# Third cross-attention of a four-layer Perceiver: the symmetric head sums in four column tiles of 32, between the next chunk's projections

## What is computed

```python
def proj(t):                       # 8 heads of 128
    return (layer_norm(t, ln_g, ln_b) @ w_in.T).reshape(Q, N, H, D).transpose(2, 0, 1, 3)
f_q, f_k, f_v = proj(q), proj(k), proj(v)          # k and v are the same context
cosine_sim = einsum('hqnd,hqmd->hqnm', f_q, f_k) / (norm(f_q)[..., None] * norm(f_k)[:, :, None])
k_ratio = 2.0 * minimum(var(f_k), 1.0) / (var(f_k) + 1.0)
var_component = einsum('hqn,hqm->hqnm', q_ratio, k_ratio)
mixed = cw * cosine_sim + vw * (cosine_sim * decorr_scale) + ww * var_component
out = einsum('hqnm,hqmd->hqnd', mixed, f_v)        # then @ w_out.T + b_out
```

## Time and profile before

| | |
|---|---|
| median of 3 runs | 2513.9 us (2513.67 to 2517.24) |
| the profiled execution's own time | 2512.27 us |
| its span | 2510.4 us |
| TensorE busy | 2241.1 us, 89% |
| VectorE busy | 1830.1 us, 73% |
| ScalarE busy | 1176.9 us, 47% |
| GpSimd busy | 520.0 us, 21% |
| mean granted TensorE clock | 0.944 |
| from the first projection of the stage to the last sums | 1421.7 to 1913.3 us of the span |

### The profile page before, as it was taken

One profiled execution on the slowest core, in us unless ns is written; L12 is line 12 of the kernel. 1 busy time (PEld: TensorE's weight loads), 2 busy tenths in 40 slices (PEclk: granted clock), 3 DMA queues, 4 the chain that ended last, 5 costly groups with the idle time before them and its releaser, 6 DMA issues. The chain is left out here.

```text
span 2510.4 us, 56943 instructions
## 1 busy us (share of the span) xinstructions
PE 2241.1 (89%) x21794; PEld 1438.2 (57%) x21794; DVE 1830.1 (73%) x2832; ACT 1176.9 (47%) x2049; POOL 520.0 (21%) x300
## 2 busy tenths in 40 slices
PE   2999979999996969999987999999998459999979
PEld 1444436666665936666666646665556425556548
DVE  6888778999996176676634488888887877777721
ACT  4566643443435337767772333333331415556542
POOL 0555540000000030000001065556662010000000
PEclk7999989999997969999998999999998769999989
DMA  8577755766745767667735322222222257777654
GB/s 282 201 242 242 261 197 148 203 200 171 206 147 179 228 154 170 161 167 172 170 71 180 128 103 103 103 102 95 75 71 62 84 131 164 157 167 176 155 142 175
DMA packets 245978, 398.00 MB, mean 159 GB/s; under 512 B 28921, under 2 KB 210305, under 8 KB 245669
## 3 DMA queue, kind: packets, MB, share of 16 engines
q1 hardware_dynamic: 240132, 393.90, 54.3%
q10 hardware_dynamic: 5664, 1.44, 0.3%
HBM read 316.44 MB, written 78.06 MB: 157 GB/s over the span
## 5 line engine op out<-in xcount | busy, mean ns | idle before, releaser
L1713 ACT ACTIVATE l1x_prob<-l1x_ring,mask_col 128x512 f32<-128x512 f32 x392 | 248.6, 690 | 113.6 <-PE l1x_ring L1805 113.3
L1629 DVE CUSTOM_DVE_ANT_0 l3x_junk<-l3x_pm,l3x_mrow,l3x_top 128x896 bf16<-128x896 f32 x224 | 247.0, 1147 | 69.5 <-PE l3x_pm L1785 64.9
L1716 ACT ACTIVATE l3x_prob<-l3x_ring 128x512 f32<-128x512 f32 x392 | 204.4, 601 | 151.9 <-PE l3x_ring L1809 150.8
L2798 POOL TENSOR_TENSOR l2x_gk<-l2x_f,first_vin 128x1024 f32<-128x1024 f32 x98 | 184.3, 1916 | 161.0 <-DVEq L2539 161.0
L1174 ACT ACTIVATE l0x_att_pt<-l0x_att_pt 128x1024 f32<-128x1024 f32 x99 | 104.7, 1058 | 167.5 <-DVE l0x_att_pt L1115 163.9
L1207 PE MATMUL l0x_att_pv<-l0x_wv,l0x_att_vin 128*128 128x512 f32 x392 | 181.9, 607 | 0.0
L2672 PE MATMUL l2x_kf<-l2w_w,l2x_nin 128*128 128x512 f32 x392 | 173.3, 602 | 4.5 <-DVE l2x_f L2513 4.5
L2672 PE MATMUL l2x_kf<-l2w_w,l2w_first 128*128 128x512 f32 x392 | 170.7, 595 | 0.0
L2513 DVE SCALAR_TENSOR_TENSOR l2x_f<-l2x_kf,l2x_rs,l2w_bias 128x1024 f32<-128x1024 f32 x98 | 125.8, 1284 | 55.5 <-PE l2x_kf L2672 43.2
L1629 DVE CUSTOM_DVE_ANT_0 l1x_junk<-l1x_pm,l1x_mrow,l1x_top 128x896 bf16<-128x896 f32 x112 | 123.7, 1148 | 55.4 <-PE l1x_pm L1785 55.4
L1629 DVE CUSTOM_DVE_ANT_0 l1x_junk<-l1x_pm,first_mrow,l1x_top 128x896 bf16<-128x896 f32 x112 | 123.4, 1147 | 49.0 <-PE l1x_pm L1785 49.0
(11 more groups left out here) (730 smaller groups left out, 4969.6 us busy)
## 6 DMA issues: line engine op xcount, KB each, us to landing
first_kt<-scratch_KS SPq DMA_DIRECT2D x84, 448.0 KB, 8.9
scratch_KT<-l0x_max_kf SPq DMA_DIRECT2D x28, 896.0 KB, 4.7
l0x_att_kt<-scratch_KT SPq DMA_DIRECT2D x56, 448.0 KB, 6.9
scratch_KS<-l0x_side_kp SPq DMA_DIRECT2D x14, 1344.0 KB, 13.4
l1x_kt<-scratch_KS SPq DMA_DIRECT2D x42, 448.0 KB, 9.2
scratch_KS<-first_kt SPq DMA_DIRECT2D x14, 1344.0 KB, 5.9
l3x_kt<-scratch_KS SPq DMA_DIRECT2D x42, 448.0 KB, 8.8
l0fw_w<-L_ffn_exp_w SPq DMA_DIRECT2D x16, 1024.0 KB, 7.9
```

The costliest lines, as they stand in the source:

```text
L1629: dve.tensor_tensor_reduce(junk[x % 2][:, :, :], pm[x % 2][:, :, 0:SPLIT], mrow[b][:, :].rearrange("p (s k) -> p s k", s=2), 1.0, top[1 - ...
L1713: ins = act.activation(into, scores, ACT.Exp, bias=R.mask_col[:, bass.ds(m * TILES + n // 4, 1)])
L1716: ins = act.activation(into, scores, ACT.Exp)
L2798: pool.tensor_tensor(gk[b][:, t, :, 0:HD], f[b][:, t, :].rearrange("p (h d) -> p h d", h=H), ks[b][:, 2, t, :].unsqueeze(2).broadcast_to([ ...
```

## The change

A head's matrix is cut at rows 32, 64 and 96 now: the strip of rows 32r to 32r + 31 takes columns from 32r on, so 130, 98, 66 and 34 columns. Each is a matmul of 128 keys x 32 columns of the array, and four heads stand in the four column tiles of 32 at once; head n of a group takes column tile (r + n) mod 4. The strips of a group go one after the other. `gather` takes a list of tiles, and `project` calls it for the chunk before: after projection 2 the sums of tile 0, after 3 those of 1 and 2, after 4 of 3, after 5 of 4 and 5, after 6 of 6. At the end more quarters have to be turned: 24 transposes, and five copies where there was one. The rest of the kernel is the same. The core of the diff:

```diff
+            TAKEN = {2: (0,), 3: (1, 2), 4: (3,), 5: (4, 5), 6: (6,)}
...
+            def width(r):
+                return GW - 32 * r
+            def sums_at(r, group):
+                first = 2 * width(r - 1) if r % 2 else 0
+                return r // 2, slice(first + group * width(r), first + (group + 1) * width(r))
+            def matrix_parts(r):
+                for n in range(4):
+                    have = slice(32 * ((r + n) % 4), 32 * ((r + n) % 4) + 32)
+                    first = 2 * width(r - 1) if r % 2 else 0
+                    yield (Msb[32 * r:32 * r + 32, n:H:4, 32 * r:],
+                           pM[have, r // 2, first:first + 2 * width(r)].rearrange("p (a n) -> p a n", a=2))
...
-                    for h in range(H // 2):
-                        for to, have in matrix_parts(h):
+                    for r in range(2):
+                        for to, have in matrix_parts(r):
                             last = dve.tensor_copy(to, have)
...
                     dve.wait_ge(S.sem("M_turned"), 1)
-                    dve.tensor_copy(Msb[HALF:HD, :, 0:HALF], pc[0:HALF, :].rearrange("p (h d) -> p h d", h=H)).then_inc(
-                        S.sem("M"), 1)
+                    dve.tensor_copy(Msb[64:96, :, 0:64], pc[0:32, :].rearrange("p (h d) -> p h d", h=H))
+                    dve.tensor_copy(Msb[96:P, 5:H, 0:96], pf[1][0:32, 1, 0:288].rearrange("p (h d) -> p h d", d=96))
+                    dve.tensor_copy(Msb[32:64, 0:7, 0:32], pf[1][0:32, 1, 288:512].rearrange(
+                        "p (h d) -> p h d", d=32)).then_inc(S.sem("M"), 1)
...
-                    for h in range(H // 2, H):
-                        for to, have in matrix_parts(h):
+                    for r in range(2, 4):
+                        for to, have in matrix_parts(r):
                             last = act.activation(to, have, ACT.Copy)
                     last.then_inc(S.sem("M_copied"), 1)
+                    act.wait_ge(S.sem("M_turned"), 1)
+                    act.activation(Msb[96:P, 0:5, 0:96], pf[1][0:32, 0, 0:480].rearrange("p (h d) -> p h d", d=96), ACT.Copy)
+                    act.activation(Msb[32:64, 7, 0:32], pf[1][0:32, 0, 480:512], ACT.Copy).then_inc(S.sem("M"), 1)
...
-                    def project(i, b, turn=False):
+                    def project(i, b, turn=False, gathered=None):
...
+                            if gathered and t in TAKEN:
+                                gather(*gathered, TAKEN[t])
...
-                            for pair in range(H // 2):
-                                for g in range(2):
-                                    h = 2 * pair + g
-                                    last = pe.matmul(pM[64 * g:64 * g + 64, pair // 2, upper(pair)],
-                                                     f[b][:, t, h * HD:h * HD + HALF], gk[b][:, t, h, :],
-                                                     start=False, stop=False, skip_group_check=True)
-                                for g in range(2):
-                                    h = 2 * pair + 1 - g
-                                    last = pe.matmul(pM[64 * g:64 * g + 64, pair // 2, lower(pair)],
-                                                     f[b][:, t, h * HD + HALF:(h + 1) * HD], gk[b][:, t, h, HALF:],
-                                                     start=False, stop=False, skip_group_check=True)
+                            for group in range(2):
+                                for r in range(4):
+                                    bank, at = sums_at(r, group)
+                                    for n in range(4):
+                                        h, to = 4 * group + n, 32 * ((r + n) % 4)
+                                        last = pe.matmul(pM[to:to + 32, bank, at],
+                                                         f[b][:, t, h * HD + 32 * r:h * HD + 32 * r + 32],
+                                                         gk[b][:, t, h, 32 * r:], start=False, stop=False,
+                                                         skip_group_check=True)
...
                         with pe.Fori(0, steps - 1) as i:
-                            project(i, 1)
-                            gather(i, 0)
-                            project(i + 1, 0)
-                            gather(i, 1)
-                    project(steps - 1, 1)
-                    gather(steps - 1, 0)
-                    gather(steps - 1, 1, query)
+                            project(i, 1, gathered=(i, 0))
+                            project(i + 1, 0, gathered=(i, 1))
+                    project(steps - 1, 1, gathered=(steps - 1, 0))
+                    gather(steps - 1, 1, beside=query)
                     pe.wait_ge(S.sem("M_copied"), 2)
-                    for h in range(H):
-                        last = pe.transpose(pc[0:HALF, h * HALF:(h + 1) * HALF], Msb[0:HALF, h, HALF:HD],
-                                            R.ident[0:HALF, 0:HALF])
+                    pe.wait_ge(S.sem("fqT"), 1)
+                    for r in range(1, 4):
+                        for h in range(H):
+                            last = pe.transpose(turned_at(r, h), Msb[0:32 * r, h, 32 * r:32 * r + 32],
+                                                R.ident[0:32 * r, 0:32 * r])
```

More of the change, by code:

```diff
@@ L2416, in use, with turned_at @@
                 return k % 2, i * TILES + k // 2
[L2418 to L2432, removed]
+            def width(r):
[9 more added lines that the diff above has]
+                           pM[have, r // 2, first:first + 2 * width(r)].rearrange("p (a n) -> p a n", a=2))
+            def turned_at(r, h):
+                if r == 1:
+                    return pf[1][0:32, 1, 288 + 32 * h:320 + 32 * h] if h < 7 else pf[1][0:32, 0, 480:512]
+                if r == 2:
+                    return pc[0:32, 64 * h:64 * h + 64]
+                return pf[1][0:32, 0, 96 * h:96 * h + 96] if h < 5 else pf[1][0:32, 1, 96 * (h - 5):96 * (h - 4)]
             def seen(h):
@@ L2704, in query, with gather @@
                             last.then_inc(S.sem("q_mean"), 1)
-                    def gather(i, b, beside=None):
-                        after(pe, S.counted(f"ratio{b}"), i + 1)
-                        for t in range(TILES):
+                    def gather(i, b, tiles=range(TILES), beside=None):
+                        if tiles[0] == 0:
+                            after(pe, S.counted(f"ratio{b}"), i + 1)
+                        for t in tiles:
                             if beside:
@@ L2711, in gather @@
                             after(pe, S.counted(f"gk{b}"), i * TILES + t + 1)
-                            for pair in range(H // 2):
-                                for g in range(2):
-                                    h = 2 * pair + g
-                                    last = pe.matmul(pM[64 * g:64 * g + 64, pair // 2, upper(pair)],
-                                                     f[b][:, t, h * HD:h * HD + HALF], gk[b][:, t, h, :],
-                                                     start=False, stop=False, skip_group_check=True)
-                                for g in range(2):
-                                    h = 2 * pair + 1 - g
-                                    last = pe.matmul(pM[64 * g:64 * g + 64, pair // 2, lower(pair)],
-                                                     f[b][:, t, h * HD + HALF:(h + 1) * HD], gk[b][:, t, h, HALF:],
-                                                     start=False, stop=False, skip_group_check=True)
-                        last.then_inc(S.counted(f"f_used{b}"), 1)
+                            for group in range(2):
[7 more added lines that the diff above has]
+                                                         skip_group_check=True)
+                        if tiles[-1] == TILES - 1:
+                            last.then_inc(S.counted(f"f_used{b}"), 1)
                     folded.wait_all(pe)
```

2 lines of the change are left out of this document (1 added, 1 removed).

## The result

The changed kernel takes 2586.5 us in the median of four runs (2585.0 to 2591.2); the kernel before, on the same chip, 2514.3 (2513.7 to 2517.2). The ratio is 1.029, with an interval of 1.028 to 1.031: **72 us slower**, where 42 were predicted (2556, range 2537 to 2585).

The account below looks back on a forecast made before the run. TensorE was taken to bound the loop, with VectorE having little to spare. Terms 27.3 + 8.4 - 1.8 - 1.5 + 3.3 + 4.5 + 1.5 = +41.7 us gave a median of 2556, range 2537 to 2585.

Parts of the forecast that it names:

- The sums themselves: Sums on TensorE in the third cross-attention's loop: 1.19 us a key tile instead of 1.354, bounds 1.14 to 1.30.
- The rival that TensorE can't be fed fast enough: Sums' short passes held to a floor between starts: 1.68 us a tile, 2596 us in all; chance 8%.
- The changes of shape: TensorE into and out of the column-tiled shape: five round trips a chunk at 0.32 us each, +1.24 a chunk.
- The new wait: Before a chunk's third projection TensorE waits for VectorE to free PSUM: 1.2 us, 3.2 at the loop's turn.
- The period: A chunk, now a loop through TensorE and VectorE, takes 35.15 us, 37.12 at the turn: +27.3 over twelve.
- From there nothing else waits: After a chunk's third projection, VectorE catches up by the last tile and GpSimd's products are ready in time.
- The cause that I named for the loss: In the loop, TensorE's wait for VectorE before the third projection, plus five changes of shape a chunk.
- The clock: Half clock on TensorE behind the six waits of 3.2 us: +4.5 us, between 0 and 6 x 2.8.
- The query: Query projection after the loop: half clock behind the 6.3 us before it costs +1.5 us (0 to 2.8).
- The assembly: Putting the matrix together after the sums, with more copies and 24 turns instead of 8: +3.3 us (1 to 5).

Follow-up runs that it names:

- a1: The changed kernel with TensorE's loop written out (no branch, same instructions in the same order): 2554.4 us in the median, +40 to the kernel before.

## Why the prediction was right about one cause and wrong in its size

*The sums themselves*: 1.19 us a tile forecast, 1.14 measured, the lower bound. The rival that TensorE can't be fed fast enough (1.68 a tile) is out in the form I gave it: 64 records in 1.14 us are 18 ns apart, counted over the four column tiles. The rule cited from the Trainium skill ("TensorE: Matmul & The Clock Gate", "Wait — 56ns, not 53.3ns?"), about 25 ns from start to start however few the columns, does not hold here when the records of all four column tiles are counted; within one column tile they start 71 ns apart, so whether it holds for a single tile no run shows. The rival's idea was right in another form: fed by fetch, such records come 3.5 us / 128 = 27 ns apart once a burst outruns what was brought ahead. The change's own groups of one or two tiles hardly ever do: one stand of 0.4 us in a1, and one of 0.9 in the last chunk of the change.

*The changes of shape*: 0.32 forecast, 0.33 measured. *The new wait*: 3.2 and 1.2 forecast, 2.96 and 0.99 measured. *The period*: 72.3 us for two chunks forecast, 71.8 measured where no branch lies in them (a1, from 1573.86 to 1645.67). The cause that I named for the loss was right, and alone it is what a1 shows: 2554.4 against 2556. That these agree to 1.6 us is partly luck: a1 lost 6.5 us by half clock behind such waits, where I took 4.5, and its shorter periods took 3 back.

*The step that failed* is "The period", and the sentence before it, "From there nothing else waits": one wait is missing in both. The prediction counted every record's time and never the **records of a turn**: 1137 became 2032, and the turn of TensorE's own loop stood in the sum at nothing, without a reason. In its place the runs showed a branch of 5.5 to 5.9 us at each of five turns, 32.5 us with the half clock behind it and less the waits that it covers. The five stands of 28.1 us cover waits of 0.98 each, so they cost 23.2, and the half clock behind them 9.3 more: the 24 records behind each took 12.1, 12.5, 12.8, 12.0 and 12.5 us instead of 10.5. The windows just behind one such stand show the clock in the third column from the end:
```profile
1534.30:1537.80 3.50, 3.46 (x5) 1.60 (x6) 0.71 (x3) 0.00 (x0) 2.62 (x2) 0.54 0.04 12
...
1658.00:1661.00 3.00, 3.00 (x4) 1.25 (x5) 2.97 (x3) 2.53 (x3) 3.00 (x3) 0.50 0.02 5
```
*The clock*: the second row lies behind one of the six waits of 2.96. Four of the six were followed by 0.50, at 1.5, 1.6, 3.0 and 3.0 us: 9.1, where I took 4.5. *The query*: 8 records in 5.34 instead of 3.63, 1.7 against 1.5.

*The assembly*: 3.3 forecast. From the last sums' end to the first product with the finished matrix it is 9.7 us (1987.16 to 1996.84) against 5.9, 3.7. Two rows of it, against the earlier trace rows; the copies take the 3.2 that were worked out:
```profile
1988.53 3.20 DVE L2575 COPY l2x_Msb<-l2x_M 32x260 f32<-32x260 f32 x8
...
1991.79 0.60 PE L2758 MATMUL l2x_kf<-ident,l2x_Msb 32*32 32x32 f32 x8 [4.63 <-DVE l2x_Msb L2575]
```
The account: 41.7 forecast, + 23.2 (branch) + 9.3 (its clock) + 4.6 (clock behind the waits) - 3.0 (sums and waits a little shorter) + 0.4 (assembly) gives 76.2 of the 79.0; 1.3 more lie before chunk 1 and 1.6 behind the stage, within what such stretches differ by from run to run. The range missed the median by 1.5 us: its bounds were those of the terms I had, and had no room for one that was absent.

## What to carry to other kernels

Count the instructions of a hardware loop's turn on TensorE, weight loads included, before cutting matmuls finer: twice as many for the same columns can push the body out of instruction memory, and then every turn pays a stand, and in 16 of 17 cases here half clock behind it. The sign is in the profile: a COMPARE_BRANCH of microseconds, idle put down to issue, and packets on the instruction queue inside a loop. A body that doesn't stay is better written out, or has its seam laid where the engine waits anyway, and its short matmuls spaced between long ones; work moved away from the end of a chunk uncovers whatever the other engine did there, so ask what was hidden before spreading it. Look also at what the DMA queues do at the seam: the stands under loads were the longer ones.

## What the runs showed that I had not expected

- A loop body of 1584 records stays in TensorE's instruction memory (branch 0.21 us, no packets in the loop); one of 2032 or 2270 does not, although the Trainium skill ("Runtime: NRT & Kernel Launch", Instruction fetch mechanics) gives TensorE room for 2048 instructions. The two packets a turn beyond the body's own could be what pushes it out; the edge between 1584 and 2032 was not tried. The same section calls the memory only two cache lines of 16 KiB; the 1584 records are more than six such blocks, and they are kept.
- The backward branch of a body that doesn't stay took 3.7 to 3.8, 3.9 to 4.3, 5.5 to 5.9 and 5.8 to 6.4 us in four kernels. The lower two are those with the sums together and the DMA queues quiet at the turn, the upper two those with the sums spread and loads under way.
- Dense 32-column matmuls start 18 ns apart for some 150 to 275 records, then TensorE stands, mostly for 2 to 4 us. At 42 ns apart (the old cut) no stand of over 0.4 us appears, written out or not.
- Waits of 2.96 us were followed by 1.2 GHz (granted clock 0.50) in four cases and not in two, in the same place of the same loop.
